# A graph layer with its five engine programs written out without loops, and its correction gathers reading their index columns in place

## The chip, the cores and the metric

The kernel runs on one core of a Trainium2 chip. The core has five engines that run programs of their own and meet only through semaphores: TensorE (PE in the rows below; its weight loads are PEld), VectorE (DVE), ScalarE (ACT), GpSimd (POOL) and SyncE (SP), and 16 DMA engines that move data between HBM and the on-chip memories. The metric is the device time of one launch in microseconds. The kernel before took 1673.95 us in the median of three runs, from 1671.81 to 1675.46.

## What is computed

There are 50,000 nodes with 512 features each and 62,500 edges sorted by destination: 50,000 of them are the self loops and 12,500 are others. The reference, cut to its core:

```
mean = segment_sum(x[src], dst) / max(degree, 1)
h = mean @ W_l + b + x @ W_r
y = x + h * sigmoid(h)
out = (y - mean(y)) / sqrt(var(y) + 1e-5)        # over the 512 features of a node
```

Most nodes have a self loop alone. For these the mean is x itself and h is `x @ (W_l + W_r) + b`. For the others a correction is added, the product of W_l with the mean of (x[src] - x[dst]).

## The kernel before

The kernel works in three stages, and all of them multiply in the same way. An f32 operand is split into a rounded part and a rest (hi and lo), and one tile of 128 rows by 512 takes twelve matmuls with 512 columns each: 4 blocks of the inner dimension times the terms hi·hi, hi·lo and lo·hi (`three`, L492 to L499). Ahead of these PE transposes the tile, four 128x128 transposes of 128 rows.

**Early stage.** The first 44 tiles of nodes ("light" later) are multiplied while DVE sorts out which edges are no self loops. Their products are kept in HBM.

**Edge stage.** 98 tiles of 128 edges each. POOL gathers x[dst] and x[src] (`xd`, `xs`, L404 to L409), DVE subtracts them (`diff`, L938), PE transposes the difference (`turn`, L559), a scan on DVE sums the runs of one destination (`sums`, L948), ACT rounds (`s_hi`, L673), DVE takes the rest (`s_lo`, L955), PE multiplies, and DVE scales and adds the bias (`c_out`, L961). SP stores the result as correction rows in HBM. The order of DVE in one tile is `c_out`, `sums`, `diff`, `s_lo`.

**Node stage.** 174 pairs of node tiles. SP loads X (L301), PE transposes it into `pT` (L592), ACT rounds to `x_hi` (L733), DVE makes `x_lo` (L998), PE runs 24 matmuls into `pH`. ACT fills `cor` with the bias (L696), POOL gathers the correction rows on top of it (L399), where a node has one, DVE adds `pH` and `cor` to `Z` (L1011), ACT applies silu (L750), DVE adds X (L1018) and takes mean and variance (`stats` L1026, `mv` L1030), POOL makes `var_eps` and `rstd` (L467, L470), DVE makes `shift` (L1037), ACT normalises into `O` (L742), SP stores (L311). In every fourth pair one of the 44 light tiles takes the same way without a product of its own.

Each engine's order is written out by hand: `node_pair(t)` on one engine issues steps of pairs t-3 to t+2. On POOL, `serve(t)` issues the gather for pair t+2 (`gather_cor`), then `make_rstd` of pair t-2, then light work. On DVE the order is `Z` of pair t-1, `stats` and `mv` of t-2, `x_lo` of t+1, the residual of t-1, `shift` of t-2, and light work.

**Loops.** `steps` (L201) writes the first eight steps of a stage out, runs the middle as a hardware loop of four steps (`looped`, L213) and writes the last ones out. In a written-out step every semaphore target and address is a constant. In a loop they come from registers, computed by register instructions, and each round ends with a compare and a branch. The edge stage has 21 rounds, the node stage 40 and the early stage some on each engine. POOL's edge gathers are written out in full.

Where POOL gathers corrections it first copies the pair's index columns out of `node_idx` into a small tile (`node_now`, L431; `l_now`, L440), waits for its own copy and then issues the indirect DMAs from it. `gate` and `dve_gate` are semaphores that nobody waits for; their increments stand as instructions of their own.

Of the kernel before, what the change touches and what calls it, by code (L numbers as in the profile page):

```python
# [6 lines left out]
def gnn_layer(nc, x, src, dst, w_l, w_r, bias, out):  # L7
# [35 lines left out]
    with ctx:  # L43
# [3 lines left out]
        def sem(name):  # L47
# [27 lines left out]
        node_now = [sb(f"node_now{b}", [P, 2], i32) for b in range(4)]  # L75
# [4 lines left out]
        l_now = sb("l_now", [P, 1], i32)  # L80
# [77 lines left out]
        gate, dve_gate = sem("gate"), sem("dve_gate")  # L158
# [17 lines left out]
        cor_reset, node_ready = sem("cor_reset"), sem("node_ready")  # L176
# [7 lines left out]
        light_in, light_now, light_reset, light_cor_in, light_z, light_silu, light_u = (  # L184
            sem("light_in"), sem("light_now"), sem("light_reset"), sem("light_cor_in"), sem("light_z"),
# [15 lines left out]
        def steps(eng, n, step):  # L201


            rounds = n // 4
            peeled(0, 8, step)
            looped(eng, 2, rounds - 1, step)
            peeled(4 * (rounds - 1), n, step)

# [3 lines left out]

        def looped(eng, first, end, step):  # L213
            with eng.Fori(first, end) as q:
                for u in range(4):
                    step(4 * q + u, q, u)
# [29 lines left out]
        def _(sp):  # L246
# [34 lines left out]
            looped(sp, 2, EARLY // 4 - 2, move_early)  # L281
# [60 lines left out]
            steps(sp, ET, edge_tile)  # L342
# [5 lines left out]
            steps(sp, NP, move)  # L348
# [10 lines left out]
        def _(pool):  # L359
# [31 lines left out]
            looped(pool, 2, FIND_ROUND, split_early)  # L391
# [34 lines left out]
            def gather_cor(t, q, u):  # L426
                nt, rows = pair_shape(t)
                b, used = ring(q, u, 4)
                wait(pool, cor_reset, t + 1)
                pool.sem_inc(gate, 1)  # L430
                g.tensor_copy(node_now[b][:, 0:nt], node_idx[:, bass.ds(EARLY + 2 * t, nt)]).then_inc(node_ready, 1)  # L431
                pool.wait_ge(node_ready, t + 1)
                pool.sem_inc(gate, 1)
                for a in range(nt):
                    gather(cor[b][0:rows, a], corr, node_now[b][0:rows, a:a + 1], rows, ET * P - 1, cor_in[b])

            def gather_light(l):
                wait(pool, light_reset, l + 1)
                pool.sem_inc(gate, 1)
                g.tensor_copy(l_now[:], node_idx[:, bass.ds(l, 1)]).then_inc(light_now, 1)  # L440
                pool.wait_ge(light_now, l + 1)
                pool.sem_inc(gate, 1)
                gather(l_cor[:], corr, l_now[:, 0:1], P, ET * P - 1, light_cor_in)

            def light_make_rstd(l):
                wait(pool, light_mv, l + 1)
                wait(pool, light_shift, l)
                wait(pool, light_normed, l)
                pool.sem_inc(gate, 1)
                g.tensor_scalar(l_var_eps[:], l_mv[:, 1:2], EPS, None, ALU.add).then_inc(light_eps, 1)  # L450
                pool.wait_ge(light_eps, l + 1)
                g.tensor_tensor(l_rstd[:], l_var_eps[:], minus_half[:, 0:1], ALU.pow).then_inc(light_rstd, 1)  # L452
# [7 lines left out]
            def make_rstd(t, q, u):  # L460
                nt, rows = pair_shape(t)
                b = u % 2
                wait(pool, mv_made, 2 * t + 2)
                wait(pool, shift_made, t - 1)
                wait(pool, normed, t - 1)
                pool.sem_inc(gate, 1)
                g.tensor_scalar(var_eps[0:rows, b, 0:nt], mv[0:rows, b, 0:nt, 1], EPS, None, ALU.add  # L467
                                ).then_inc(eps_added, 1)
                pool.wait_ge(eps_added, t + 1)
                g.tensor_tensor(rstd[0:rows, b, 0:nt], var_eps[0:rows, b, 0:nt], minus_half[0:rows, 0:nt], ALU.pow  # L470
                                ).then_inc(rstd_made, 1)
# [9 lines left out]
            steps(pool, NP, serve)  # L481
# [6 lines left out]
        def _(pe):  # L488
# [31 lines left out]
            looped(pe, 2, MERGE_ROUND, early_tile)  # L520
# [14 lines left out]
            looped(pe, MERGE_ROUND, FIND_ROUND, early_tile)  # L535
# [69 lines left out]
            steps(pe, ET, edge_tile)  # L605
# [17 lines left out]
            steps(pe, NP, node_pair)  # L623
# [3 lines left out]
        def _(act):  # L627
# [38 lines left out]
            looped(act, 2, EARLY // 4 - 1, early_tile)  # L666
# [58 lines left out]
            steps(act, ET, edge_tile)  # L725
# [50 lines left out]
            steps(act, NP, node_pair)  # L776
# [9 lines left out]
        def _(dve):  # L786
# [204 lines left out]
            steps(dve, ET, edge_tile)  # L991
# [29 lines left out]
            def moments(t, q, u):  # L1021
                nt, rows = pair_shape(t)
                wait(dve, u_made, t + 1)
                wait(dve, rstd_made, t - 1)
                for a in range(nt):
                    v.bn_stats(stats[0:rows, u % 2, a], Z[0:rows, u % 4, a]).then_inc(stats_made, 1)  # L1026
                wait(dve, stats_made, 2 * t + nt)
                dve.sem_inc(dve_gate, 1)
                for a in range(nt):
                    v.bn_aggr(mv[0:rows, u % 2, a], stats[0:rows, u % 2, a]).then_inc(mv_made, 3 - nt)  # L1030
# [19 lines left out]
            def light_moments(l):  # L1050
# [4 lines left out]
                dve.sem_inc(dve_gate, 1)  # L1055
# [28 lines left out]
            steps(dve, NP, node_pair)  # L1084
# [30 lines left out]
```

## Time and profile before

| | value |
|---|---|
| median of the runs | 1673.95 us |
| the profiled execution | 1673.7 us, span 1671.9 us |
| PE, PEld busy | 1602.2 us (96%), 1315.8 us |
| DVE, ACT, POOL busy | 1413.4, 1035.4, 1015.3 us |
| mean granted TensorE clock | 0.990 |
| instructions in the span | 30356 |
| DMA | 349.26 MB, 209 GB/s |

A busy share says how long an engine had an instruction in it. Matmuls overlap their neighbours, so PE's 96% hides short pauses; the distance between equal steps of two tiles shows them. Three stretches follow one another: to about 168 us the early stage, from 181 to 517 us the edge stage, then the node stage to the end.

### The profile page before, as it was taken

The numbers are of one execution on the slowest core, as the hardware profiler recorded it, in microseconds if no ns is written. First come the engines' busy times: TensorE is split into PE (matmuls) and PEld (weight loads), VectorE is DVE, ScalarE is ACT, GpSimd is POOL, SyncE is SP. The second block draws the span as 40 slices with busy tenths as digits, with TensorE's granted clock in tenths as the row PEclk, the third lists the DMA queues.
The fourth block names the chain that finished last, engine by engine and source line by source line (L and its number), as shares of the span: only waits on it lengthen the run. The fifth ranks groups of instructions, "written<-read, shape, count | busy, mean of one in ns | idle before, by whom it ended". The sixth has DMA issues, their size and how long they took to land.

```text
span 1671.9 us, 30356 instructions
## 1 busy us (share of the span) xinstructions
PE 1602.2 (96%) x7886; PEld 1315.8 (79%) x7886; DVE 1413.4 (85%) x2174; ACT 1035.4 (62%) x1433; POOL 1015.3 (61%) x1307
## 2 busy tenths in 40 slices
PE   7998899999999999999999999999999999999995
PEld 5887677777778788888878888887888888888884
DVE  7888899989995888888888888888888888888886
ACT  4443333333334677777767767777777776777775
POOL 6445555555553666666666666666666666666664
PEclk9999999999999999999999999999999999999998
DMA  5445688878884666656666666665666666666664
GB/s 182 148 163 175 190 255 248 254 233 249 254 242 141 197 203 209 227 195 223 202 200 227 197 220 209 211 223 191 211 216 205 226 199 220 208 202 224 199 221 158
DMA packets 204144, 349.26 MB, mean 209 GB/s; under 512 B 37020, under 2 KB 51126, under 8 KB 204117
## 3 DMA queue, kind: packets, MB, share of 16 engines
q1 hardware_dynamic: 156135, 274.22, 49.1%
q0 software_dynamic: 46944, 74.22, 16.6%
q10 hardware_dynamic: 1038, 0.50, 0.1%
q8 instruction: 11, 0.18, 0.0%
q14 instruction: 16, 0.13, 0.0%
HBM read 288.78 MB, written 139.67 MB: 256 GB/s over the span
## 4 chain that ended last, share of the span: by engine, by line
issue 28%; PE 27%; POOL 19%; DVE 12%; ACT 9%; POOLq 2%; DVEq 1%; DMA 1%; SPq 0%; ACTq 0%
PE pH L498 23%; POOL cor L399 6%; ACT O L742 4%; DVE Z L1011 4%; DVE stats L1026 3%; POOL rstd L470 3%; POOL light_cor L399 3%; PE pT L566 2%; POOL l_var_eps L450 2%; ACT cor L696 2%; POOL var_eps L467 2%; ACT light_o L759 2%; DVE l_stats L1053 2%; POOL l_rstd L452 1%; PE pT L507 1%
## 5 line engine op out<-in xcount | busy, mean ns | idle before, releaser
L498 PE MATMUL pH<-ws_hi,x_hi 128*128 128x512 f32 x1564 | 631.5, 404 | 21.2 <-issue 14.6
L498 PE MATMUL pH<-ws_hi,x_lo 128*128 128x512 f32 x1564 | 613.8, 392 | 0.0
L498 PE MATMUL pH<-ws_lo,x_hi 128*128 128x512 f32 x1564 | 611.7, 391 | 0.0
L399 POOL DMA_INDIRECT cor<-correction_rows,node_now x347 | 370.6, 1068 | 215.5 <-POOL node_now L431 148.5
L498 PEld LDWEIGHTS pH<-ws_hi,x_hi 128*128 128x128 f32 x1564 | 295.3, 189 | 85.6 <-issue 30.8
L750 ACT ACTIVATE Z<-Z 128x1024 f32<-128x1024 f32 x174 | 184.2, 1059 | 284.7 <-DVE Z L1011 174.2
L498 PEld LDWEIGHTS pH<-ws_hi,x_lo 128*128 128x128 f32 x1564 | 294.9, 189 | 64.5
L498 PEld LDWEIGHTS pH<-ws_lo,x_hi 128*128 128x128 f32 x1564 | 295.7, 189 | 55.3
L742 ACT ACTIVATE O<-Z,shift,rstd 128x512 f32<-128x512 f32 x347 | 261.4, 801 | 3.7 <-DVE shift L1037 3.7
L1011 DVE TENSOR_TENSOR Z<-pH,cor 128x1024 f32<-128x1024 f32 x174 | 212.0, 1218 | 35.7 <-issue 23.8
L1026 DVE BATCH_NORM_STATS2 stats<-Z 128x6 f32<-128x512 f32 x347 | 221.5, 680 | 0.0
L1018 DVE TENSOR_TENSOR Z<-Z,X 128x1024 f32<-128x1024 f32 x174 | 213.2, 1226 | 0.0
L998 DVE TENSOR_TENSOR x_lo<-pT,x_hi 128x1024 fp32r<-128x1024 f32 x174 | 207.3, 1191 | 2.4 <-ACT x_hi L733 2.4
L733 ACT ACTIVATE x_hi<-pT 128x1024 fp32r<-128x1024 f32 x174 | 175.2, 1007 | 33.2 <-PE pT L592 18.5
L696 ACT ACTIVATE cor<-bias_rows 128x1024 f32<-128x1024 f32 x174 | 181.6, 1044 | 0.0
L592 PEld LDWEIGHTS pT<-eye,X 128*128 128x128 f32 (+1 forms) x1388 | 161.1, 140 | 24.8 <-DMA X<-in_x 2.9
L592 PE MATMUL pT<-eye,X 128*128 128x128 f32 (+1 forms) x1388 | 179.8, 272 | 0.7 <-DMA X<-in_x 0.6
L470 POOL TENSOR_TENSOR rstd<-var_eps,minus_half 128x2 f32<-128x2 f32 x174 | 171.3, 984 | 14.5
L673 ACT ACTIVATE s_hi<-sums 128x512 fp32r<-128x512 f32 x98 | 62.0, 633 | 190.3 <-DVE sums L948 113.7
L498 PE MATMUL pH<-wl_hi,s_hi 128*128 128x512 f32 x392 | 163.8, 418 | 2.8 <-issue 0.6
L399 POOL DMA_INDIRECT xd<-in_x,dst_idx x98 | 98.9, 1009 | 109.7 <-issue 92.0
L498 PE MATMUL pH<-wl_lo,s_hi 128*128 128x512 f32 x392 | 154.9, 395 | 0.0
(134 smaller groups left out, 1834.1 us busy)
## 6 DMA issues: line engine op xcount, KB each, us to landing
X<-in_x SPq DMA_DIRECT2D x173, 512.0 KB
out<-O SPq DMA_DIRECT2D x173, 512.0 KB
correction_rows<-c_out SPq DMA_DIRECT2D x98, 256.0 KB
light_x<-in_x SPq DMA_DIRECT2D x66, 256.0 KB, 2.6
light_h<-early_product SPq DMA_DIRECT2D x44, 256.0 KB
out<-light_o SPq DMA_DIRECT2D x44, 256.0 KB
join_row<-joined SPq DMA_DIRECT2D x98, 64.0 KB
light_h<-in_x SPq DMA_DIRECT2D x22, 256.0 KB, 2.7
```

The costliest lines, as they stand in the source:

```text
L399: g.indirect_dma_start(out=out_, out_offset=None, in_=table, in_offset=bass.IndirectOffsetOnAxis(ap=idx, axis=0), bounds_check=bound, oob_ ...
L470: g.tensor_tensor(rstd[0:rows, b, 0:nt], var_eps[0:rows, b, 0:nt], minus_half[0:rows, 0:nt], ALU.pow).then_inc(rstd_made, 1)
L498: last = mm(ps, a[:, k], w[:, k], start=(n == 0), stop=(n == len(terms) - 1))
L592: last = nc.tensor.transpose(pT[u % 2][:, a, k * P:k * P + rows], X[0:rows, b, a, k * P:(k + 1) * P], eye[0:rows, 0:rows])
L696: a_(cor[u][:], bias_rows[:].rearrange("p (a n) -> p a n", a=1).to_broadcast([P, 2, D]), ACT.Copy).then_inc(cor_reset, 1)
L733: a_(x_hi[b][:, 0:nt, :, 0:rows], pT[b][:, 0:nt].rearrange("p a (k r) -> p a k r", k=K)[:, :, :, 0:rows], ACT.Copy).then_inc(hi_made, 1)
L742: last = a_(O[0:rows, b, a], Z[0:rows, u % 4, a], ACT.Identity, scale=rstd[0:rows, b, a:a + 1], bias=shift[0:rows, b, a:a + 1])
L750: a_(Z[0:rows, b, 0:nt], Z[0:rows, b, 0:nt], ACT.Silu).then_inc(silu_made, 1)
L998: v.tensor_tensor(x_lo[b][:, 0:nt, :, 0:rows], pT[b][:, 0:nt].rearrange("p a (k r) -> p a k r", k=K)[:, :, :, 0:rows], x_hi[b][:, 0:nt, :, ...
L1011: v.tensor_tensor(Z[0:rows, b, 0:nt], pH[u % 2][0:rows, 0:nt], cor[b][0:rows, 0:nt], ALU.add).then_inc(z_made, 1)
L1018: v.tensor_tensor(Z[0:rows, b, 0:nt], Z[0:rows, b, 0:nt], X[0:rows, b, 0:nt], ALU.add).then_inc(u_made, 1)
L1026: v.bn_stats(stats[0:rows, u % 2, a], Z[0:rows, u % 4, a]).then_inc(stats_made, 1)
```

## The change

All calls of `looped` and `steps` become `peeled`, so that each of the five programs is one straight list with constants. The indirect DMAs for corrections take their indices directly from the column of `node_idx`, as the edge gathers already take theirs from `dst_idx` and `src_idx`; the copies, the waits for them and the increments of `gate` and `dve_gate` go. No operation on data other than those copies is added, removed or moved against another of its engine. Cut to its core:

```
-        def steps(eng, n, step):
-            rounds = n // 4
-            peeled(0, 8, step)
-            looped(eng, 2, rounds - 1, step)
-            peeled(4 * (rounds - 1), n, step)
...
-            steps(sp, ET, edge_tile)
+            peeled(0, ET, edge_tile)
...
-            steps(sp, NP, move)
+            peeled(0, NP, move)
...
-            looped(pool, 2, FIND_ROUND, split_early)
+            peeled(8, 4 * FIND_ROUND, split_early)
...
                 wait(pool, cor_reset, t + 1)
-                pool.sem_inc(gate, 1)
-                g.tensor_copy(node_now[b][:, 0:nt], node_idx[:, bass.ds(EARLY + 2 * t, nt)]).then_inc(node_ready, 1)
-                pool.wait_ge(node_ready, t + 1)
-                pool.sem_inc(gate, 1)
                 for a in range(nt):
-                    gather(cor[b][0:rows, a], corr, node_now[b][0:rows, a:a + 1], rows, ET * P - 1, cor_in[b])
+                    n = EARLY + 2 * t + a
+                    gather(cor[b][0:rows, a], corr, node_idx[0:rows, n:n + 1], rows, ET * P - 1, cor_in[b])
...
                 wait(pool, light_reset, l + 1)
-                pool.sem_inc(gate, 1)
-                g.tensor_copy(l_now[:], node_idx[:, bass.ds(l, 1)]).then_inc(light_now, 1)
-                pool.wait_ge(light_now, l + 1)
-                pool.sem_inc(gate, 1)
-                gather(l_cor[:], corr, l_now[:, 0:1], P, ET * P - 1, light_cor_in)
+                gather(l_cor[:], corr, node_idx[:, l:l + 1], P, ET * P - 1, light_cor_in)
...
                 wait(dve, stats_made, 2 * t + nt)
-                dve.sem_inc(dve_gate, 1)
```

The same replacement of `steps` and `looped` stands on PE, ACT, DVE and POOL. What it does to the instruction lists is seen at two places.

POOL in the node stage, the second half of a round, before. `ISA` and `REGISTER_ALU` rows compute addresses and semaphore targets in registers.

```order
L431 COPY node_now<-node_idx 128x2
L399 DMA cor<-correction_rows,node_now 128x512 [waits node_ready]
L399 DMA cor<-correction_rows,node_now 128x512
L199 ISA
L467 TENSOR_SCALAR var_eps<-mv 128x2 [waits normed,mv_made,shift_made]
L469 REGISTER_ALU
L470 TENSOR_TENSOR rstd<-var_eps,minus_half 128x2 [waits eps_added]
L199 REGISTER_ALU
L440 ISA [waits light_reset]
L440 COPY l_now<-node_idx 128x1
L399 DMA light_cor<-correction_rows,l_now 128x512 [waits light_now]
```

The same place now (its lines are numbered by the changed file: L383 is the gather, L442 and L445 are `var_eps` and `rstd`):

```order
L383 DMA cor<-correction_rows,node_idx 128x512 [waits cor_reset]
L383 DMA cor<-correction_rows,node_idx 128x512
L442 TENSOR_SCALAR var_eps<-mv 128x2 [waits normed,shift_made,mv_made]
L445 TENSOR_TENSOR rstd<-var_eps,minus_half 128x2 [waits eps_added]
L383 DMA light_cor<-correction_rows,node_idx 128x512 [waits light_reset]
```

The copies and register rows are gone; a gather waits only for the bias that ACT writes under it.

DVE in the edge stage, the last tile of a round and the turn to the next, before:

```order
L199 ISA [waits c_product]
L961 ISA [waits c_stored0]
L961 SCALAR_TENSOR_TENSOR c_out<-pH,rdeg,bias_rows 128x512
L199 REGISTER_ALU
L948 SCALAR_TENSOR_TENSOR sums<-mask,pT 128x520 [waits s_lo_made,mask_made,s_hi_made,carried,turned]
L938 TENSOR_TENSOR diff<-xs,xd 128x512 [waits turned,xd_in2,xs_in2]
L955 TENSOR_TENSOR s_lo<-sums,s_hi 128x512 [waits c_product,s_hi_made]
L214 REGISTER_ALU
L214 COMPARE_AND_BRANCH
```

The same place now (L936, L923, L913 and L930 are `c_out`, `sums`, `diff` and `s_lo`):

```order
L936 SCALAR_TENSOR_TENSOR c_out<-pH,rdeg,bias_rows 128x512 [waits c_stored0,c_product]
L923 SCALAR_TENSOR_TENSOR sums<-mask,pT 128x520 [waits s_lo_made,mask_made,s_hi_made,carried,turned]
L913 TENSOR_TENSOR diff<-xs,xd 128x512 [waits turned,xd_in2,xs_in2]
L930 TENSOR_TENSOR s_lo<-sums,s_hi 128x512 [waits c_product,s_hi_made]
```

The operations and their order are the same; the waits stand at them with constants, as in the first eight tiles of the stage before.

## Rows read from the trace of the kernel before

**Rows 1.** The page: busy time by engine and instruction queues (packets, MB, share).
```profile
PE 1602.2 (96%) x7886; PEld 1315.8 (79%) x7886; DVE 1413.4 (85%) x2174; ACT 1035.4 (62%) x1433; POOL 1015.3 (61%) x1307
...
q8 instruction: 11, 0.18, 0.0%
q14 instruction: 16, 0.13, 0.0%
```

**Rows 2.** Timeline, PE, edge stage: start us, us, engine line op, times [idle before <-releaser].
```profile
201.90 0.60 PE L566 MATMUL pT<-eye,diff 128*128 128x128 f32 x4
...
208.37 0.60 PE L566 MATMUL pT<-eye,diff 128*128 128x128 f32 x4
...
275.98 0.60 PE L566 MATMUL pT<-eye,diff 128*128 128x128 f32 x4
276.66 0.50 PE L498 MATMUL pH<-wl_hi,s_hi 128*128 128x512 f32 x1
...
282.80 0.60 PE L566 MATMUL pT<-eye,diff 128*128 128x128 f32 x4
...
492.94 0.60 PE L566 MATMUL pT<-eye,diff 128*128 128x128 f32 x4
```

**Rows 3.** Timeline, PE, edge stage, the pause near 364 us.
```profile
367.11 0.66 PE L566 MATMUL pT<-eye,diff 128*128 128x128 f32 x4 [2.74 <-DVE diff L938]
```

**Rows 4.** Timeline, DVE, edge stage: a written-out tile and a looped one.
```profile
202.10 0.75 DVE L961 SCALAR_TENSOR_TENSOR c_out<-pH,rdeg,bias_rows 128x512 f32<-128x512 f32 x1
...
279.96 0.75 DVE L961 SCALAR_TENSOR_TENSOR c_out<-pH,rdeg,bias_rows 128x512 f32<-128x512 f32 x1 [0.24 <-PE pH L498]
```

**Rows 5.** Timeline, PE, node stage: its start, a free stretch, a round, its end.
```profile
522.84 1.03 PE L592 MATMUL pT<-eye,X 128*128 128x128 f32 x8
...
546.18 0.47 PE L498 MATMUL pH<-ws_hi,x_hi 128*128 128x512 f32 x1 [3.29 <-DVE x_lo L998]
...
566.18 1.03 PE L592 MATMUL pT<-eye,X 128*128 128x128 f32 x8
...
572.52 1.04 PE L592 MATMUL pT<-eye,X 128*128 128x128 f32 x8
...
894.78 0.47 PE L498 MATMUL pH<-ws_hi,x_hi 128*128 128x512 f32 x1 [0.38 <-issue]
...
920.76 0.47 PE L498 MATMUL pH<-ws_hi,x_hi 128*128 128x512 f32 x1 [0.31 <-issue]
...
1631.04 1.04 PE L592 MATMUL pT<-eye,X 128*128 128x128 f32 x8
```

**Rows 6.** Timeline, DVE, the turn of a round in the node stage.
```profile
915.03 0.16 DVE L1037 SCALAR_TENSOR_TENSOR shift<-mv,rstd 128x2 f32<-128x2 f32 x1 [0.92 <-POOL rstd L470]
...
916.73 1.22 DVE L1011 TENSOR_TENSOR Z<-pH,cor 128x1024 f32<-128x1024 f32 x1 [0.59 <-issue]
...
919.47 1.19 DVE L998 TENSOR_TENSOR x_lo<-pT,x_hi 128x1024 fp32r<-128x1024 f32 x1
```

**Rows 7.** Waits of DVE and of POOL: us in total, times, longest.
```profile
DVE shift L1037 <- POOL rstd L470: 81.1, 91, 5.4
...
DVE Z L1011 <- issue: 23.8, 40, 0.7
...
POOL cor L399 <- POOL node_now L431: 148.5, 168, 1.0
...
POOL node_now L431 <- ACT cor L696: 61.0, 42, 1.5
```

**Rows 8.** Timeline, POOL, node stage: one pair, and the pause near 1145 us.
```profile
911.52 1.03 POOL L399 DMA_INDIRECT cor<-correction_rows,node_now  x1 [0.87 <-POOL node_now L431]
912.85 1.00 POOL L399 DMA_INDIRECT cor<-correction_rows,node_now  x1 [0.30 <-issue]
...
1147.85 1.02 POOL L399 DMA_INDIRECT cor<-correction_rows,node_now  x1 [3.45 <-issue]
```

**Rows 9.** One line's instructions (L399): count, ns least/median/most.
```profile
L399 POOL DMA_INDIRECT xd<-in_x,dst_idx x98: 992/997/1464, 122.7 to 493.1; - x98
```

More of the change, by code:

```diff
@@ L74, in gnn_layer @@
         node_idx = sb("node_idx", [P, NTILES + 1], i32)
-        node_now = [sb(f"node_now{b}", [P, 2], i32) for b in range(4)]
         l_x, l_h, l_cor, l_z, l_u, l_o = (sb(f"light_{n}", [P, D], f32) for n in ("x", "h", "cor", "z", "u", "o"))
@@ L79, in gnn_layer @@
         l_var_eps, l_rstd, l_shift = sb("l_var_eps", [P, 1], f32), sb("l_rstd", [P, 1], f32), sb("l_shift", [P, 1], f32)
-        l_now = sb("l_now", [P, 1], i32)
         e_x, e_t, e_out = (l_x, l_h), (l_cor, l_z), (l_u, l_o)
@@ L155, in gnn_layer @@
         idx_ready = sem("idx_ready")
-        gate, dve_gate = sem("gate"), sem("dve_gate")
         xs_in = [sem(f"xs_in{b}") for b in range(4)]
@@ L175, in gnn_layer @@
             sem("shift_made"), sem("normed"))
-        cor_reset, node_ready = sem("cor_reset"), sem("node_ready")
+        cor_reset = sem("cor_reset")
         stored = [sem(f"stored{b}") for b in range(2)]
@@ L183, in gnn_layer @@
             sem("early_done"), sem("early_kept"))
-        light_in, light_now, light_reset, light_cor_in, light_z, light_silu, light_u = (
-            sem("light_in"), sem("light_now"), sem("light_reset"), sem("light_cor_in"), sem("light_z"),
+        light_in, light_reset, light_cor_in, light_z, light_silu, light_u = (
+            sem("light_in"), sem("light_reset"), sem("light_cor_in"), sem("light_z"),
             sem("light_silu"), sem("light_u_made"))
@@ L211, in peeled @@
                 step(t, t // 4, t % 4)
[L213 to L216, printed above, removed]
         def light_tail(light, first, end):
@@ L280, in _ @@
             peeled(0, 8, move_early)
-            looped(sp, 2, EARLY // 4 - 2, move_early)
+            peeled(8, EARLY - 8, move_early)
             sp.wait_ge(list_made, 1)
@@ L448, in light_make_rstd @@
                 wait(pool, light_normed, l)
-                pool.sem_inc(gate, 1)
                 g.tensor_scalar(l_var_eps[:], l_mv[:, 1:2], EPS, None, ALU.add).then_inc(light_eps, 1)
@@ L465, in make_rstd @@
                 wait(pool, normed, t - 1)
-                pool.sem_inc(gate, 1)
                 g.tensor_scalar(var_eps[0:rows, b, 0:nt], mv[0:rows, b, 0:nt, 1], EPS, None, ALU.add
@@ L480, in serve @@
                 light(q, u)
-            steps(pool, NP, serve)
+            peeled(0, NP, serve)
             single(NP - 2, make_rstd)
@@ L519, in _ @@
             peeled(0, 8, early_tile)
-            looped(pe, 2, MERGE_ROUND, early_tile)
+            peeled(8, 4 * MERGE_ROUND, early_tile)
             def merge(bank, rows):
@@ L534, in _ @@
                 merge(pH[1][:, a, :], rowed_f[:, a * CH:(a + 1) * CH]).then_inc(merged, 1)
-            looped(pe, MERGE_ROUND, FIND_ROUND, early_tile)
+            peeled(4 * MERGE_ROUND, 4 * FIND_ROUND, early_tile)
             pe.wait_ge(dst_found, 1)
@@ L604, in edge_tile @@
                 three(pH[b][:, 0, :], s_hi[b], s_lo[b], wl_hi, wl_lo).then_inc(c_product, 1)
-            steps(pe, ET, edge_tile)
+            peeled(0, ET, edge_tile)
             pe.wait_ge(early_kept, EARLY)
@@ L622, in node_pair @@
                 last.then_inc(product, 1)
-            steps(pe, NP, node_pair)
+            peeled(0, NP, node_pair)
         @block.scalar
@@ L665, in _ @@
             peeled(1, 8, early_tile)
-            looped(act, 2, EARLY // 4 - 1, early_tile)
+            peeled(8, EARLY - 4, early_tile)
             def round_sums(t, q, u):
@@ L724, in edge_tile @@
                     single(1, reset_cor)
-            steps(act, ET, edge_tile)
+            peeled(0, ET, edge_tile)
             def round_x(t, q, u):
@@ L775, in node_pair @@
                 shifted(t, q, u, -3, NP, normalise)
-            steps(act, NP, node_pair)
+            peeled(0, NP, node_pair)
             single(NP - 3, normalise)
@@ L990, in edge_tile @@
                     find_nodes()
-            steps(dve, ET, edge_tile)
+            peeled(0, ET, edge_tile)
             def split_x(t, q, u):
@@ L1054, in light_moments @@
                 wait(dve, light_stats, l + 1)
-                dve.sem_inc(dve_gate, 1)
                 v.bn_aggr(l_mv[:], l_stats[:]).then_inc(light_mv, 1)
@@ L1083, in node_pair @@
                 light(q, u)
-            steps(dve, NP, node_pair)
+            peeled(0, NP, node_pair)
             single(NP - 1, add_cor)
```

## The prediction, made before the changed kernel ran

> **What bounds the kernel now.** I read the page first: PE is busy 96% of the span, DVE 85%, the others near 60% [rows 1]. That makes PE the engine to follow, but its busy share cannot show short pauses, since matmuls overlap. So the second view is PE's timeline, read as a pace: the distance between the transposes of two tiles that follow each other. In the edge stage the tiles that are written out keep 3.235 us (201.90 to 208.37 are two tiles), the looped ones need 6.82 for two, 3.41 each [rows 2]. In the node stage the written-out pairs keep 6.34 us (566.18 to 572.52), while a looped round of four takes 25.98, which is 0.62 more than 4 x 6.34 [rows 5]. The same matmuls at the same clock run in both forms, so 3.235 and 6.34 are PE's own pace, and what lies above them is waiting.
>
> The third view is DVE's timeline, for who is late. In the node stage PE's first matmul of the new round starts at 920.76 [rows 5], and DVE's `x_lo` ends at 919.47 + 1.19 = 920.66 [rows 6]: PE waits for it, though its row says "issue", since the wait is a sequencer instruction of its own. Ahead of that `x_lo` DVE stood still twice: 0.92 us for POOL's `rstd` and 0.59 us at the turn of the round [rows 6]. The waits say how regular that is: 23.8 us in 40 times before `Z`, one for each of the 40 rounds, and 81.1 us in 91 times for `rstd` [rows 7]. In the edge stage PE and DVE are a closed pair: matmuls of a tile need `s_lo`, and `c_out` needs the matmuls. Written out, `c_out` starts at 202.10 with no idle time; looped, it starts after 0.24 us more [rows 4], and PE's matmuls at 276.66 come only 0.68 us after the tile's first transpose [rows 2]. The order shows register instructions between a semaphore and the operation that it frees.
>
> **The edge stage.** From 208.37 to 492.94 there are 83 tiles in 284.57 us [rows 2]. At 3.235 they would take 268.5, so 16.1 us are above the pace. Of these about 3 us belong to one pause, in which PE stood for 2.74 us [rows 3]; nothing in the change speaks to it, and I leave it in. The other 13.0 us go. They are the two delays just named, every second tile, and in the first eight tiles, where POOL, ACT and SP do the same work, they are absent. What is late next is PE itself, or DVE's chain, which has practically the same length as PE's two tiles. That is the tightest point of the forecast: with DVE at 3.24 a tile there is no cover for any new cost on DVE. The bounds of this term are 0, if the chain stays at 3.4 for a reason that I don't see, and 16, if the pause goes too.
>
> **The node stage.** From 522.84 to 1631.04 there are 169 pairs in 1108.20 us [rows 5]. At 6.34 they would take 1071.5, so 36.7 us are above the pace. About 30 rounds show the regular 0.62 (19 us); the rest is five disturbances of 2 to 5 us.
> The regular part: DVE loses the 0.59 at the turn. POOL's part of the chain shortens as well: each gather of a pair begins 0.87 us after the end of a copy of 0.19, and the second one 0.30 after the first [rows 8]. Without copy the first gather follows what POOL did before like the second does, so 1.06 - 0.30 = 0.76 us go per pair, and once more in a round for the light tile: 3.8 us of 25.98. Of the 148.5 us of idle time behind copies [rows 7] most turn into slack, because POOL then waits for ACT's bias, as it did before 61.0 us long [rows 7]. `rstd` comes up to 0.76 earlier per pair and DVE's 0.92 shrinks to nearly nothing. PE needs only 0.62 of the 1.5 us; the whole regular part goes.
> The first disturbance is PE's 3.29 us for `x_lo` at 546 [rows 5]: POOL starts the stage late, behind the stores of corrections, and does five pairs of gathers ahead of its first `rstd`. Five or six copies with their idle time, some 0.76 each, are 4 us earlier; the wait for ACT's bias gives a part back. I take this pause down to about 1.
> Three others come with POOL standing still before a gather, 3.45 us in the one shown [rows 8]; there are three, 106 gathers apart each time. That even spacing is a property of the gathers, whose number is unchanged, so these stay; with more slack on POOL they reach PE only in part. I keep 5 us for them and 1.7 for the rest of the start: 36.7 - 6.7 = 30.0 us go. Bounds: 0, if POOL's lateness alone set the regular part and stays; 36.7.
>
> **Costs that the trace does not show.** The index read in place: `xd` is gathered from a column of a wide tile today and takes 997 ns in the median [rows 9], the correction gathers 1.00 to 1.03 us from their copies [rows 8]. Between 0.1 less and 0.1 more each; I take zero, and POOL, idle for 39% of the span [rows 1], would cover either.
> The length of the programs: PE alone executes 7886 matmuls and as many weight loads [rows 1]; with their waits that is a list of some 16,400 instructions, where before it was 2,835 (loads counted). Queue q8 brought 0.18 MB in 11 packets [rows 1], which is 64 bytes an instruction and 256 of them in a packet; the new list needs 64 packets. All five lists grow from 4,800 to 24,600 instructions, from 0.31 MB [rows 1] to 1.6 MB. As bytes that is nothing beside 349 MB. As a stall it is free as far as the trace goes: pair 6 and 7 of the node stage, at the end of eight written-out pairs (512 instructions of PE, so two packets), still run at 6.34 [rows 5]. Above, the bound is any stall per packet; I take 0.
> The Trainium skill (Runtime: NRT & Kernel Launch, Instruction fetch mechanics) says that the sequencer fetches the next 16 KiB block while it runs the present one, and that crossing is mostly hidden. No run here has yet shown a list of this length.
> The early stage has the same loops, but PE's tiles there keep one pace except where they wait for sorting; I take 0, bounds -1 and 1.
> Data, queues and buffers are as before; SP's DMAs come in the same order, and SP waits for DVE most of the time. With tiles 4% closer in the edge stage the same bytes move 4% faster.
>
> **Sum.** 1673.7 (the profiled execution, 1.8 above its span) - 13.0 - 30.0 = 1630.7, and the runs' median is 0.25 above that execution. I forecast **1631 us**.
>
> **Rivals.**
> *Part of the gain meets a new wait* (chance 0.24). For it: DVE's chain in the edge stage is as long as PE's two tiles, and ACT idles for `Z` in nearly every pair. If half of each term stays: 1673.7 - 6.5 - 15 = 1652.
> *The round's turn was not what held DVE* (0.06). POOL's `rstd` alone sets the regular 0.62 in the node stage and still comes late, as ACT's bias gates the gathers anyway; only the edge stage gains: 1673.7 - 13 = 1661. Against it: 1.5 us of idle time stood ahead of an `x_lo` that was 0.62 late.
> The Trainium skill (Advanced Engine Details and Errata, Control Flow Timing) gives a compare and branch about 108 ns. By it 61 rounds would be worth 6.6 us, estimated from that page, against 13 and 30 by the rows; the row of 0.59 us at each turn speaks against so small a price.
> *Slower: straight code starves PE* (0.06). The place is PE's sequencer at each block of 256 instructions; before, the loops ran again from what had been fetched. The price is a stall for each of 64 packets, and the 43 us are used up from 0.67 us a packet on. At 1 us it would be 1630.7 + 64 = 1695. For it: the fetches share the DMA engines with 209 GB/s. Against it: a packet lasts PE some 25 us, and the written-out pairs above.
> *The change does nothing that counts* (0.02): the fetched columns or the constants make no difference, 1673.
>
> **How the numbers follow.** The forecast's own case has 0.62 and reaches from 1622 (the pauses go too) to 1644. The range of 8 in 10 takes in the half gain: **1621 to 1657**. Within 0.2%, about 3.3 us, is what a measurement can hardly tell from no change. Faster by more: 0.62 + 0.24 + 0.06 = 0.92. The same: 0.02. Slower: 0.06.
>
> **What would show it.** Transposes 3.23 to 3.25 us apart through all of the edge stage, and `c_out` without idle time. In the node stage 6.34 apart without a step every fourth pair; no idle time before `Z` put down to issue; `shift` waiting for `rstd` far under 81 us, and more of POOL's idle time ended by ACT's bias. The pause at the start of the node stage near 1 us. Three or four pauses of POOL, 106 gathers apart, still there. Instruction packets about 64 on q8, and PE without steps at them. I am wrong if PE's pace stays above 6.4 or 3.3, or if steps in it follow the packets.

## The result, and the profile after

The changed kernel takes 1616.49 us (median of 4 runs, 1616.14 to 1617.37) against 1674.05 us for the kernel before (median of 4, 1671.81 to 1675.46). The ratio is 0.9661, with a 95% interval of 0.9649 to 0.9674: 57.6 us less, 14.5 us below the forecast of 1631 and 4.5 us below the lower end of its range. The profiled execution took 1616.76 us, its span is 1615.0 us. One of the four executions of e1 below took 2676 us at a mean granted clock of 0.558: its median counts it, its ratio goes by the other three.

The page of the changed kernel: busy time by engine, the two instruction queues, and the chain that ended last, by engine.
```profile
PE 1574.8 (98%) x7886; PEld 1311.1 (81%) x7886; DVE 1408.7 (87%) x2174; ACT 1028.8 (64%) x1433; POOL 947.9 (59%) x1089
...
q8 instruction: 64, 1.05, 0.3%
...
q14 instruction: 64, 0.52, 0.1%
...
PE 95%; DVE 2%; DMA 1%; issue 1%; SPq 0%; ACT 0%; POOL 0%; POOLq 0%; DVEq 0%
```
Against [rows 1], PE's busy time fell by 27 us, POOL's by 67 (218 copies are gone). PE's queue q8 brings 64 packets, as forecast. The chain that ended last now lies on PE for 95% of the span. The same row of the page before, which the prediction didn't read, had PE at 27% although PE was busy for 96%:
```profile
issue 28%; PE 27%; POOL 19%; DVE 12%; ACT 9%; POOLq 2%; DVEq 1%; DMA 1%; SPq 0%; ACTq 0%
```

PE's timeline in the edge and in the node stage, the places that answer to [rows 2, 5]: start us, us, engine line op.
```profile
206.66 0.60 PE L541 MATMUL pT<-eye,diff 128*128 128x128 f32 x4
...
281.18 0.60 PE L541 MATMUL pT<-eye,diff 128*128 128x128 f32 x4
281.54 0.48 PE L473 MATMUL pH<-wl_hi,s_hi 128*128 128x512 f32 x1
...
476.21 0.60 PE L541 MATMUL pT<-eye,diff 128*128 128x128 f32 x4
...
505.92 1.03 PE L567 MATMUL pT<-eye,X 128*128 128x128 f32 x8
512.26 1.03 PE L567 MATMUL pT<-eye,X 128*128 128x128 f32 x8
...
899.00 1.03 PE L567 MATMUL pT<-eye,X 128*128 128x128 f32 x8
905.34 1.03 PE L567 MATMUL pT<-eye,X 128*128 128x128 f32 x8
...
1577.38 1.03 PE L567 MATMUL pT<-eye,X 128*128 128x128 f32 x8
```
In the edge stage the matmuls follow a transpose after 0.36 us, no longer 0.68, and the same 83 tiles take 269.55 us instead of 284.57. In the node stage the same 169 pairs take 1071.46 us instead of 1108.20: 6.340 each, without a single step, neither at the start of the stage nor where POOL stands still nor, with 64 instruction packets over the span, anywhere else.

DVE's timeline in the edge stage, one `c_out`:
```profile
278.15 0.75 DVE L936 SCALAR_TENSOR_TENSOR c_out<-pH,rdeg,bias_rows 128x512 f32<-128x512 f32 x1
```
POOL's timeline in the node stage, a gather after a usual wait and one behind a long pause:
```profile
798.54 0.99 POOL L383 DMA_INDIRECT cor<-correction_rows,node_idx  x1 [1.17 <-ACT cor L671]
...
806.32 1.14 POOL L383 DMA_INDIRECT cor<-correction_rows,node_idx  x1 [4.41 <-issue]
```
`c_out` starts without idle time, where it had 0.24 us [rows 4]. The gather read from the wide tile still takes 1.0 us [rows 8]. POOL still stands still before one gather in 106 (at 806.32 and at 1105.33; a third time, for 1.95 us, at 1403.49), and PE's timeline is smooth there.

The waits from 517 to 1600 us: us in total, times, longest.
```profile
ACT x_hi L708 <- PE pT L567: 263.8, 170, 2.4
POOL cor L383 <- ACT cor L671: 229.8, 117, 3.0
DVE Z L986 <- PE pH L473: 94.6, 157, 0.7
POOL cor L383 <- issue: 80.8, 221, 4.4
...
DVE shift L1011 <- POOL rstd L445: 9.2, 8, 2.0
```
Over the whole span `shift` waits 11 us for `rstd` where it waited 81 (9 and 76 in these limits), the 40 waits of `Z` for "issue" are gone, and ACT and DVE now wait for PE [rows 7].

**Where the 56.9 us between the two profiled executions lie.** Edge stage: 284.57 - 269.55 = 15.0. Node stage: 1108.20 - 1071.46 = 36.7. Before the edge stretch: 208.37 - 206.66 = 1.7. Between the stretches: 0.2. From the last row (1631.04 and 1577.38) to the end of the execution (1673.7 and 1616.76): 42.7 - 39.4 = 3.3. Against the forecast's 43.0 these are 2.0, 6.7, 1.7, 0.2 and 3.3 us more.

### The profile page after: what moved, and what is told of

Same layout as the page of the kernel before. It is cut to its first block, busy times and chain, and to the rows that moved or that the text cites. A ratio compares the mean times of both kernels' runs of the same rounds, so it can differ in the third digit from the quotient of the medians.

```text
span 1615.0 us, 24709 instructions
## 1 busy us (share of the span) xinstructions
PE 1574.8 (98%) x7886; PEld 1311.1 (81%) x7886; DVE 1408.7 (87%) x2174; ACT 1028.8 (64%) x1433; POOL 947.9 (59%) x1089
## 4 chain that ended last, share of the span: by engine, by line
PE 95%; DVE 2%; DMA 1%; issue 1%; SPq 0%; ACT 0%; POOL 0%; POOLq 0%; DVEq 0%
PE pH L473 81%; PE pT L567 9%; PE pT L541 3%; PE pT L482 1%; DMA light_h<-in_x 0%; DVE w_sum L799 0%; DVE w_sum L794 0%; DVE sums L923 0%; DMA light_x<-in_x 0%; PE pH L500 0%; PE pH L503 0%; DVE stats L1001 0%; SPq L246 0%; DVE row_mask L790 0%; DVE Z L794 0%
## 5 line engine op out<-in xcount | busy, mean ns | idle before, releaser
L383 POOL DMA_INDIRECT cor<-correction_rows,node_idx x347 | 366.2, 1055 | 313.3 <-ACT cor L671 229.8
L567 PE MATMUL pT<-eye,X 128*128 128x128 f32 (+1 forms) x1388 | 179.5, 272 | 0.0
L473 PE MATMUL pH<-wl_hi,s_lo 128*128 128x512 f32 x392 | 155.0, 396 | 0.0
L383 POOL DMA_INDIRECT xd<-in_x,dst_idx x98 | 99.2, 1012 | 93.3 <-DVE diff L913 90.4
```

What stands on the lines that cost most here:

```text
L383: g.indirect_dma_start(out=out_, out_offset=None, in_=table, in_offset=bass.IndirectOffsetOnAxis(ap=idx, axis=0), bounds_check=bound, oob_ ...
L473: last = mm(ps, a[:, k], w[:, k], start=(n == 0), stop=(n == len(terms) - 1))
L567: last = nc.tensor.transpose(pT[u % 2][:, a, k * P:k * P + rows], X[0:rows, b, a, k * P:(k + 1) * P], eye[0:rows, 0:rows])
```

## The experiments

Sixteen kernels were run in four groups (e1 to e4, e5 to e8, and so on), each beside the kernel before on the same chip (1672.60, 1676.42, 1675.34 and 1674.88 us there). "Us" is the median of the runs. In the table "edge" is the time of 97 tiles' distances in that stage and "node" that of 345 tiles' (172.5 pairs), both worked out from the starts of PE's matmuls in the one profiled execution of each kernel; "a round" is what four pairs take above PE's own 25.36 us, in the median of the rounds from the fourth on.

| kernel | us | ratio (95%) | edge | node | a round |
|---|---|---|---|---|---|
| before | 1674.05 | | 332.5 | 1129.5 | 0.62 |
| changed | 1616.49 | 0.966 (0.965-0.967) | 317.0 | 1092.8 | 0 |
| e1_copies_kept | 1626.74 | 0.973 (0.971-0.975) | 317.3 | 1100.6 | 0 |
| e2_edge_only | 1648.24 | 0.986 (0.984-0.987) | 316.5 | 1121.0 | 0.46 |
| e3_node_only | 1630.18 | 0.975 (0.973-0.976) | 330.4 | 1092.8 | 0 |
| e4_early_only | 1672.47 | 1.000 (0.999-1.001) | 329.2 | 1131.9 | 0.62 |
| e5_pool_node | 1636.01 | 0.975 (0.973-0.977) | 332.9 | 1092.8 | 0 |
| e6_dve_looped | 1625.70 | 0.969 (0.967-0.972) | 326.3 | 1092.8 | 0 |
| e7_pe_looped | 1621.88 | 0.967 (0.965-0.969) | 323.9 | 1092.8 | 0 |
| e8_dve_only | 1664.46 | 0.993 (0.990-0.995) | 321.9 | 1130.8 | 0.66 |
| e9_gates | 1618.04 | 0.966 (0.964-0.967) | 318.1 | 1092.8 | 0 |
| e10_pool_copies | 1683.50 | 1.005 (1.003-1.006) | 332.2 | 1136.5 | 0.94 |
| e11_two_copies | 1667.43 | 0.995 (0.993-0.997) | 317.2 | 1137.1 | 0.70 |
| e12_four_c_out | 1617.88 | 0.965 (0.963-0.967) | 317.8 | 1092.8 | 0 |
| e13_copy_ahead | 1643.62 | 0.982 (0.980-0.983) | 332.1 | 1102.1 | 0 |
| e14_pool_dve | 1651.94 | 0.986 (0.985-0.988) | 332.2 | 1110.2 | 0 to 0.7 |
| e15_pool_act | 1680.97 | 1.004 (1.002-1.005) | 332.4 | 1138.1 | 0.93 |
| e16_pool_dve_act | 1652.54 | 0.987 (0.985-0.988) | 332.2 | 1108.2 | 0 to 0.7 |

### Which stage, and whether the copies or the loops

e1: the changed kernel with the copies back, and with the increments of `gate` and `dve_gate` (not shown here; e9 below has them alone).
```diff
-                    gather(cor[b][0:rows, a], corr, node_idx[0:rows, n:n + 1], rows, ET * P - 1, cor_in[b])
+                g.tensor_copy(node_now[b][:, 0:nt], node_idx[:, bass.ds(EARLY + 2 * t, nt)]).then_inc(node_ready, 1)
+                pool.wait_ge(node_ready, t + 1)
+                    gather(cor[b][0:rows, a], corr, node_now[b][0:rows, a:a + 1], rows, ET * P - 1, cor_in[b])
```
Expected: 

> All five programs written out, but POOL still copies the index columns (two copies' worth of work a round more than the changed kernel: one per pair and one per light tile, about 0.76 us of POOL each). Theory 1 (the loops' turns and registers set the regular loss of PE, the copies only bring the pauses at the start of the node stage and behind POOL's long pauses to PE): node pace 6.34 with no step each fourth pair, but start and three pauses back, some 8 us: about 1624. Rival 2 (the copies are free once the loops are gone): 1616 to 1618. Rival 3 (the copies are what makes rstd late): the 0.62 us of each round back too, 1616 + 19 + 8 = 1643.

Measured 1626.74 (its profiled execution 1624.0). PE's loss in the node stage is 6.4 us in two steps at the start and 1.4 us behind two of POOL's long pauses; the 0.6 a round is gone. Theory 1 holds.

e2, e3 and e4 write out one stage each, on every engine that loops in it; e3 also reads the index in place. One line of e2:
```diff
-            steps(dve, ET, edge_tile)
+            peeled(0, ET, edge_tile)
...
```
Expected of e2: 

> Only the edge stage is written out, on SP, PE, ACT and DVE; early and node stage are loops as before, copies kept. Theory 1 (each stage's gain is its own): 97 distances of tiles in about 317 us instead of 332.5, so 1674 - 15.5 = 1658.5, node stage as before with all its disturbances. Rival 2 (the 3.2 us pause at 361 us was the kernel's own and only the fully straight program loses it): 320 in the stage, 1661.7. Rival 3 (the written-out code costs where fetches of the looped stages and the straight one mix): above 1662.

Expected of e3: 

> Only the node stage is written out, on all five engines, and its gathers read the index in place; early and edge stage are loops as before. Theory 1: the node stage loses 36.8 us and the tail 1 to 3: 1674 - 38 = 1636, with no disturbance of PE in the stage although POOL's three long pauses are there. Rival 2 (the pauses were absorbed because the earlier stages brought POOL ahead): start pause of about 3 us and some of the others back, 1640 to 1646.

Expected of e4: 

> Only the early stage is written out; edge and node stage are loops as before, copies kept. It is also a second profile of the looped stages. Theory 1: the first matmul of the edge stage comes 1.4 us earlier, 1672.6; the 3.2 us pause near 361 us doesn't come back in the same place (a single event of one execution), the start pause and the three behind POOL's long pauses do, with the drops of the granted clock behind them. Rival 2: early stage worth nothing, 1674, and the pause at 361 stands where it stood (a property of the kernel).

e3 came as theory 1 has it, 4 us better against the kernel before on its chip (42 us for 38): its edge stage, looped as before, lacks the pause near 361 and starts 1.6 us earlier. e4 is worth nothing that the timing can tell; its profile shows the pauses of the looped stages where they were, without the 3.2 us near 361. e2 gained 24 us instead of 15: the edge stage gave its 16, and the loop of the node stage, though its text is the same, lost only 0.46 us a round. `Z` stood 19.3 us in 39 times for "issue" there, 0.49 each, where the kernel before has 23.8 in 40, 0.59 each [rows 7]. The same turn of the same loop costs DVE 0.1 us less in the program whose edge stage is written out ahead of it. Why is open.

### Which engine

e5 writes out POOL alone in the node stage and drops its copies; e8 writes out DVE alone, in both stages; e6 and e7 are the changed kernel with one engine's loops kept. One call of each:
```diff
 e5
-            steps(pool, NP, serve)
+            peeled(0, NP, serve)
...
 e8
-            steps(dve, NP, node_pair)
+            peeled(0, NP, node_pair)
...
```
Expected of e5: 

> Only POOL's part of the node stage is written out, with the index read in place; every other engine and stage is a loop as before. Theory 1 (DVE's turn of the round sets the regular loss, POOL's copies only carry the pauses to PE): the pauses at the start and behind POOL's three long pauses go, some 10 us, the regular 0.6 us a round stays: 1673 - 10 = 1663. Rival 2 (POOL's late rstd sets the regular loss): it goes as well, 25 us more: 1638.

Expected of e6: 

> The changed kernel with DVE alone kept in loops in the edge and the node stage. Theory 1 (DVE's turn and DVE's register instructions hold PE): node stage 0.4 to 0.6 us above 4 x 6.34 in each of 41 rounds, edge stage near 3.4 a tile: 1616 + 20 + 13 = 1649. Rival 2 (the turn fits into the slack that rstd left behind when it came early, so that only both together cost): node stage at 6.34, edge stage alone back, 1616 + 13 = 1629 or less.

Expected of e7: 

> The changed kernel with PE alone kept in loops, in all three stages; its list of instructions is short again. Theory 1 (PE's own registers and turn cost a few tenths of a us where it has just waited, and nothing where it is the late one): up to 0.1 us a tile in the edge stage and 0.1 to 0.3 a round in the node stage, 1616 + 5 to 15 = 1621 to 1631. Rival 2 (PE's loop costs nothing, the other engines set everything): 1616 to 1618. Rival 3 (the long list of PE cost something by its fetches that the looped PE saves): below 1615.

Expected of e8: 

> The kernel before with DVE alone written out in the edge and the node stage; the other engines keep loops, POOL keeps its copies. Theory 1: most of the edge stage's 13 us goes (0.24 ahead of c_out), and in the node stage the 0.59 at the turn goes, the pauses stay: 1673 - 10 - 20 = 1643. Rival 2 (POOL's rstd and the turn share one stall, so that taking one away shows the other): node stage keeps its 0.6 a round, 1663.

This is where my theory fell. e5, with four engines still in loops, has the changed kernel's node stage to 0.1 us: rival 2, 1636 against its 1638. e8 leaves the node stage as it was. The waits of e8 (560 to 1590 us) show one stall gone and the other grown:
```profile
DVE shift L1037 <- POOL rstd L470: 107.3, 79, 3.5
...
DVE Z L1011 <- issue: 0.3, 1, 0.3
```
The kernel before has 67.6 us and 23.2 us there, together 90.8. e6 is its rival 2 (the edge stage's 9 us back, the node stage untouched: 1626, where the rival had 1629 or less). e7 is theory 1 in the edge stage and rival 2 in the node stage. In the edge stage the registers do cost: without its pause of 2.1 us DVE's loop is worth 7 us there, and PE's 0.13 us each fourth tile, 3 us.

### Why the copies decide

The chain of waits of the kernel before, from 700 to 726 us (start us, us, what), says what I had not read: it closes on itself without PE. The 1.60 us of "issue" are `rstd`, which runs on until 724.40; short pieces are left out.
```profile
699.46 1.14 POOL light_cor L399
700.62 0.20 POOL node_now L431
...
700.96 0.51 issue
...
703.01 1.00 POOL cor L399
...
704.43 0.73 POOL rstd L470
705.27 0.70 DVE l_stats L1053
...
706.89 0.07 DVE Z L1011
...
708.04 1.29 DVE stats L1026 x2
...
711.04 1.00 POOL l_var_eps L450
...
713.09 1.24 DVE Z L1011
...
715.32 0.80 ACT light_o L759
...
717.53 0.96 ACT cor L696
...
718.74 0.19 POOL node_now L431
719.07 0.51 issue
...
722.61 0.05 POOL rstd L470
...
722.78 1.60 issue
724.38 0.19 POOL l_now L440
...
725.44 1.14 POOL light_cor L399
```
From one gather of the light tile to the next are 725.44 - 699.46 = 25.98 us, the round that PE shows [rows 5], and no piece of it is PE's: POOL's `rstd` frees DVE, whose moments free POOL's next `var_eps` and `rstd`; behind these DVE comes to `Z`, that frees ACT, whose bias frees POOL's next gathers, and `rstd` stands behind the gathers. The copies and the 0.5 us of "issue" behind each lie on this chain. PE needs 25.36 a round and follows. The timelines bear it out: from the ninth pair of the stage to the 165th `Z` never starts less than 0.5 us after the end of the last matmul that it reads, in the median 2.1 to 3.5 us by the pair's place in the round; in the changed kernel 0.04. e10, e11 and e13 to e16 test the chain.

The chain holds one more piece that I had not seen when I planned these runs, and no run takes it out alone. Timelines of the kernel before, POOL and then DVE:
```profile
716.54 0.72 POOL L470 TENSOR_TENSOR rstd<-var_eps,minus_half 128x2 f32<-128x2 f32 x1
...
722.61 1.79 POOL L470 TENSOR_TENSOR rstd<-var_eps,minus_half 128x2 f32<-128x2 f32 x1
...
722.60 1.22 DVE L1018 TENSOR_TENSOR Z<-Z,X 128x1024 f32<-128x1024 f32 x1
```
The same of e10, DVE and then POOL:
```profile
705.06 1.22 DVE L1018 TENSOR_TENSOR Z<-Z,X 128x1024 f32<-128x1024 f32 x1
...
705.14 2.00 POOL L399 DMA_INDIRECT cor<-correction_rows,node_now  x1 [0.30 <-issue]
```
A POOL operation that starts while DVE adds X to `Z` (L1018) takes longer (all counts from 560 to 1590 us). In the kernel before one `rstd` a round does (38 of them take 1.79 us in the median instead of 0.72), and it lies on the chain; in the changed kernel none does. In e8 a gather does as well, 40 times, 2.05 us instead of 1.0; in e10 a gather in place of the `rstd`. The border is sharp: 37 gathers of the kernel before start 0.01 to 0.03 us behind the beginning of an addition and keep their 1.0 us, the 40 of e8 start 0.03 to 0.35 us behind it and don't. So a shift of a few hundredths of a us between POOL and DVE puts 1.0 us into the chain or takes it out.

e10 and e11 put copies where theory said they matter (of e11 the second copy alone):
```diff
 e10 (the kernel before)
-            steps(pool, NP, serve)
+            peeled(0, NP, serve)
 e11 (e1, with a second copy behind the first)
...
+                g.tensor_copy(node_now[b][:, 0:nt], node_idx[:, bass.ds(EARLY + 2 * t, nt)]).then_inc(node_ready, 1)
+                pool.wait_ge(node_ready, 2 * t + 2)
```
Expected of e10: 

> Only POOL's part of the node stage is written out, and it keeps its copies of the index columns. Theory 1, formed after the last runs (POOL's chain alone holds the node stage; its loop code makes the regular 0.6 us of each round, its copies the pauses at the start and behind POOL's long pauses): node stage 173 intervals in about 1100 us as in the fully written-out kernel with copies, 1636 + 8 = 1644. Rival 2 (the copies carry most of the regular part as long as the other engines loop): 1110 to 1125 us in the stage, 1655 to 1668.

Expected of e11: 

> All programs written out, and POOL copies the index columns of each pair twice, the second copy after a wait for the first. One copy with its wait was worth 0.76 us of POOL a pair and 8 us in all, through pauses alone. Theory 1 (POOL has room of some 1 us a pair; what a copy costs is only how much of a disturbance reaches PE): two copies eat the room, a regular loss in each pair or round appears, 0.2 to 0.8 us a round, 1626 + 10 to 30 = 1636 to 1656. Rival 2 (room is much wider): pauses only, 1632.

e10 missed on every side: it is slower than the kernel before, 1.0047 (1.0030 to 1.0064). So with the copies kept POOL's loop code is not what costs, and e5's gain needs the copies gone. e10's trace says where its loss sits: each of its rounds from the third to the 23rd has a gather of some 2.0 us and nearly all lose about 0.9; the four rounds behind the long pause near 1161 us have none and lose nothing. e11 missed too, by 11 us above its range: one more copy in a program without any loop brings back 0.70 us a round and the pauses, 41 us; its trace has 40 long `rstd` and 39 long gathers. The first copy cost 10 (e1 against the changed kernel). As long as the chain is shorter than PE's round, a link on it costs nothing regular; what one costs beyond that isn't its own length alone, as e8 and e10 show.

e13 takes the link out and leaves the work: all loops are kept, and the copy is made a pair ahead, behind `rstd`. The order of POOL's steps:
```diff
             def serve(t, q, u):
                 shifted(t, q, u, 2, NP, gather_cor)
                 shifted(t, q, u, -2, NP, make_rstd)
+                if fixed(t) and t == 1:
+                    pool.wait_ge(cor_in[0], 32)
+                shifted(t, q, u, 3, NP, copy_idx)
```
Expected: 

> The looped kernel before, all loops kept, but POOL's copy of a pair's index columns is made one pair ahead, behind rstd, so that a gather finds it ready; the light tile's copy stays where it was. Theory 1 (a closed chain POOL - DVE - ACT - POOL of 25.98 us a round holds the node stage, and the copies count because the 0.87 us between a copy and its gather stand on it): the chain falls under PE's 25.36, node stage 1093 to 1100 us, about 1636 to 1643 like the kernel whose POOL has no copies. Rival 2 (what counts is POOL's work and semaphores as a whole, wherever the copy stands): 0.3 to 0.6 a round stay, 1655 to 1673.

Measured 1643.62, a round at 25.36, node stage 1102.1: theory 1, 2 us above its bound for the stage. DVE's turn is still there, 24.0 us in 40 times before `Z`, and costs PE nothing. POOL's timeline of e13 shows the gather of the pair no longer behind its copy.
```profile
712.62 1.14 POOL L399 DMA_INDIRECT cor<-correction_rows,node_now  x1 [1.20 <-ACT cor L703]
714.06 1.00 POOL L399 DMA_INDIRECT cor<-correction_rows,node_now  x1 [0.30 <-issue]
...
716.11 0.95 POOL L428 COPY node_now<-node_idx 128x2 int32 x1
```
What it lacks against e5 are the disturbances: 2.5 us at the start and two of POOL's long pauses. e13 changes two things at once: the copy is off the gather's way, and now the copy is what meets DVE's addition (118 copies take 0.98 us in the median instead of 0.17), while no `rstd` is lengthened any more. Which of the two brings the round down is open.

e14, e15 and e16 ask whose turns stand on the chain: e10 with DVE, with ACT, with both written out in the node stage.

Expected of e14: 

> Node stage: POOL and DVE written out, copies kept; PE, ACT and SP loop; the rest as before. POOL alone so gave 1683, DVE alone (with the edge stage) 1664, all five together lost nothing regular. Theory 1 (DVE's turn of 0.59 stands on the closed chain and goes, POOL's order of waits is what remains): 0.92 - 0.5 = about 0.4 us a round, 1660. Rival 2 (all of the turns must go together, ACT's among them): 0.9 a round, 1680. Rival 3: nothing regular left, 1643.

Expected of e15: 

> Node stage: POOL and ACT written out, copies kept; PE, DVE and SP loop; the rest as before. Theory 1 (ACT's turn stands between its O and the bias that POOL's gather waits for, once a round): as much below 1683 as ACT's turn is long, 0.3 to 0.6 us a round, 1658 to 1670. Rival 2 (DVE's turn is the one on the chain): 1683.

Expected of e16: 

> Node stage: POOL, DVE and ACT written out, copies kept; PE and SP loop; the rest as before. Theory 1 (the closed chain holds only these three engines, and PE and SP are not on it): nothing regular left, as in the fully written-out kernel with copies, node stage about 1100 us, 1643. Rival 2 (PE's turn is part of it): 0.2 to 0.6 a round stay, 1652 to 1668.

DVE's loop stands on the chain (e10's 43.7 us above PE's pace in the stage become 17.4), ACT's does not (45.3), and both together do as DVE's alone (15.4). e14 lies halfway between its theory 1 (1660) and rival 3 (1643); e15 is rival 2. For e16 neither: 8 us remain above theory 1, half of them in single rounds that lose up to 0.7 and half behind a long pause of POOL. With e8 this says that the parts don't add up: DVE's loop is worth nothing while POOL loops, and 26 us once it doesn't. The lengthened POOL operations go with it: 24 long gathers and 29 long `rstd` in e14 and 16 and 23 in e16, against 40 and 36 in e8. This is read from the traces; no run moves the addition and nothing else, so that it is the reason isn't shown.

### Two side questions

e9 puts back the dropped increments of `gate` and `dve_gate`; e12 gives `c_out` four buffers. DVE's wait in e12:
```diff
 e12
-                b, used = ring(q, u, 2)
+                b, used = ring(q, u, 4)
                 wait(dve, c_product, t + 1)
                 wait(dve, c_stored[b], 16 * used)
```
Expected of e9: 

> The changed kernel with the semaphore increments gate and dve_gate put back that the change had dropped beside the copies (one before each gather pair and each var_eps on POOL, one before each mv on DVE); otherwise a repetition of it. Theory 1 (they cost nothing): 1616.5 within 2, node stage at 1092.8. Rival 2 (each costs its engine some 0.1 us): node stage still at PE's pace, since POOL and DVE have room, the same time. A pause of 1 to 3.5 us of PE near the 52nd store of the edge stage may come or not; where the kernels of this call all show it, it belongs to the chip or the profiling and not to the form of the program.

Expected of e12: 

> The changed kernel with four buffers for c_out in place of two, so that DVE waits for the store of four tiles ago. Theory 1 (the pause of 1.4 to 3.5 us near the 52nd store, seen in half of the profiled executions, is DVE waiting for a store that landed some 5 us late): the pause can't reach PE any more, 1616 or up to 3 less, edge stage at most 317 us. Rival 2 (something else stops PE there): where the repetition of this call shows the pause, this one does as well.

The increments cost nothing: 0.9655 of the kernel before, against 0.9661. The pause at the 52nd store (some 3 us in the kernel before, e5, e7, e10 and e13 to e16, 1 to 2 in e6, e8, e9, e11 and e12, under 0.5 in e1 to e4 and in the changed kernel's own profile) came in e9 and in e12 alike, 1.0 and 1.1 us, so it is no wait for a store of `c_out`; rival 2. e1 to e4 ran on one chip, and there even the looped edge stages of e3 and e4 lack it; on the chips where it came it is longest with that stage in loops (3.4 to 3.6 us in e5, e10 and e13 to e16) and 1.0 to 1.1 with it written out (e9, e11, e12). With one profile of each kernel, chip and execution can't be told apart. Its cause is open.

## Why the prediction was too cautious

**Where the time would go** was right: edge and node stage, each to PE's own pace, nothing for the long programs, nothing for the index in place, and the signs announced for it are there, but for the pause of about 1 us at the start of the node stage, which is gone altogether. The direction and the likeliest case came. What failed is the terms that were kept, and one cause.

**Edge stage, 13.0 of 16.1.** Measured 15.0. That "nothing in the change speaks to" the pause of PE [rows 3] was no reason to leave it in: e3 and e4, with the same loops in that stage, don't have it. That it was absent is luck as far as the runs show. It makes some 3.1 us of the 15.0, so the regular part gave 11.9 of the 13.0, and e6, e7 and e8 confirm the two delays named.

**Node stage, the regular part.** The size was right and the cause only half. I let two stalls of DVE add up, 0.59 us at the turn and 0.92 for `rstd` [rows 6]. e8 removes the first and changes nothing; e5 and e13 keep DVE's loop and gain all of the regular part. The rival "the round's turn was not what held DVE" (chance 0.06) came nearer to the cause, but concluded that `rstd` would still come late, and 1661 was the wrong end. The Trainium skill (Advanced Engine Details and Errata, Control Flow Timing) prices a compare and branch at about 108 ns; by the rows here a turn of this loop costs DVE 0.49 to 0.59 us, and DVE's loop costs PE anything from nothing (e6) to 26 us in all (e10 against e14) in this stage, which no price for a branch can tell.

**Node stage, 6.7 us kept.** This is the step that failed: "with more slack on POOL they reach PE only in part. I keep 5 us for them and 1.7 for the rest of the start". Nothing reached PE: of the 6.7 us none was left. POOL's pauses are still there, 106 gathers apart, as forecast; but I had given POOL 0.76 us of slack a pair without asking how much a chain at 25.98 gains when it falls well under 25.36. e1 shows that all of this term hangs on the copies: with them 7.8 us return, without them none. Together with the edge stage's pause and the end of the kernel, for which there was no term, this puts the result below the range.

**What was taken as zero.** The edge stretch begins 1.7 us earlier; I had given the early stage bounds of 1. The end is 3.3 us shorter, and the forecast had no term for it: before, the chain of waits over the last 32 us ran through POOL, DVE and ACT without PE, since the closed chain and not PE ended the stage; now PE is on it until 1596.03, 19 us from the end. e5 (19.9 us from the last tile's first matmul to the end, against 22.1 before and 22.1 in e10) fits that it comes with the node stage's chain.

**The long program.** 64 packets of q8 and not one step of PE at them; the Trainium skill (Runtime: NRT & Kernel Launch, Instruction fetch mechanics) says that crossing a block is mostly hidden, and the trace agrees. e7, whose PE keeps 11 packets, is no faster.

## What to carry to other kernels

Before pricing a stall at the engine where it shows, read the chain of waits over one round and ask whether the bound engine is on it. Here the page's row of the chain by engine gave the hint: 27% for an engine that was busy for 96%. If a closed chain of other engines is longer than the bound engine's own round, the stall shows at the bound engine but its links lie elsewhere; once it is shorter, its links cost nothing regular, and the slack swallows disturbances as well. Don't add up the links' lengths: a link taken out (DVE's turn in e8, POOL's loop in e10) brought nothing or less in the node stage. By the traces that is because it moved the engines against each other, which no run has shown by itself. Making a small copy one pair earlier brought 31 us without touching a loop, more than half of the whole change's 57.6.

## What the runs showed of the hardware

- The same loop, word for word, costs DVE 0.49 us at its turn in e2 and 0.59 us in the kernel before, which differ in the edge stage ahead of it alone.
- A POOL operation that starts more than 0.03 us into DVE's addition of two 128x1024 f32 tiles (`Z<-Z,X`, 1.22 us) takes longer, and what is left of its time behind the addition's end is constant for each kind: `rstd` 0.59 us (1.79 us in all instead of 0.72, 38 times in the kernel before; for `rstd` the border lies 0.03 us ahead of the addition), a gather 0.87 (2.05 instead of 1.0, 40 times in e8), a copy of indices 0.04 (0.98 instead of 0.17, 118 times in e13).
- An indirect gather directly behind a POOL copy whose result it reads starts 0.85 to 0.91 us after the copy's end nearly always, in loops and in straight code alike; made a pair ahead, the copy costs only its own time.
- The two drops of PE's granted clock in the node stage before (0.5, so 1.2 GHz, for 3.41 us at 547 and at 1158 us, each behind a stall of PE there) are absent in the changed kernel, whose clock stays at 1.0, 2.4 GHz, from 179.5 to 1602.9 us.
- 64 packets of instructions for PE in 1615 us go with no step in its timeline.
